# A transformer layer with int4 feed-forward weights: the first gate weights prepared one stage earlier, and the down-weight pieces of the last pair moved to the first pairs

## The reference

```python
x = x + layernorm(attention(layernorm(x)))        # x: 2048 tokens x 1024, 32 heads, 8 key/value groups
def ffn(x, gate_Wq, up_Wq, down_Wq, scales, zeros):
    # int4 weights, two to a word, one scale and one zero for 64 inputs
    Wg, Wu, Wd = dequantize(gate), dequantize(up), dequantize(down)
    g = einsum('bsh,ih->bsi', x, Wg)               # inter = 2752
    u = einsum('bsh,ih->bsi', x, Wu)
    return einsum('bsi,hi->bsh', silu(g) * u, Wd)
x = x + layernorm(ffn(layernorm(x)))
```

## Time and profile before

| | |
|---|---|
| median of 3 runs | 2761.49 us (2760.53 to 2762.55) |
| the profiled execution's own time | 2762.64 us |
| its span, first to last instruction | 2760.9 us |
| PE, busy | 2634.7 us, 95% |
| DVE, busy | 1602.5 us, 58% |
| POOL, busy | 1175.7 us, 43% |
| ACT, busy | 952.5 us, 34% |
| gate and up | from 1449 us to 2289 us |

### The profile page before, as it was taken

The page is one execution under the profiler, slowest core; times in us unless marked ns, Lnnn a source line. Parts: engine busy times, 40 slices in busy tenths (PEclk is TensorE's granted clock), DMA queues, the critical chain, the costliest instruction groups (busy, mean ns, idle before and its releaser), DMA issues. The chain is left out here.

```text
span 2760.9 us, 42122 instructions
## 1 busy us (share of the span) xinstructions
PE 2634.7 (95%) x17064; PEld 1116.0 (40%) x17064; DVE 1602.5 (58%) x1986; ACT 952.5 (34%) x1674; POOL 1175.7 (43%) x654
## 2 busy tenths in 40 slices
PE   6999899999999999988978999999999998999998
PEld 3445533333333333324443444444444443444443
DVE  6332778778787787815677688777777770101001
ACT  3111366666666666661112223233222220000000
POOL 0000177777777777781222334555555550100001
PEclk8999999999999999999988999999999998999999
DMA  4223101011010110003223222333333347332220
GB/s 171 81 76 97 30 17 30 22 40 30 17 30 24 38 30 2 1 1 145 91 76 107 91 76 90 112 106 111 101 113 108 106 152 254 110 105 71 71 71 30
DMA packets 180252, 209.67 MB, mean 76 GB/s; under 512 B 17649, under 2 KB 138737, under 8 KB 180081
## 3 DMA queue, kind: packets, MB, share of 16 engines
q1 hardware_dynamic: 175440, 198.11, 22.2%
q10 hardware_dynamic: 4640, 9.18, 0.9%
HBM read 146.01 MB, written 61.08 MB: 75 GB/s over the span
## 5 line engine op out<-in xcount | busy, mean ns | idle before, releaser
L734 POOL TENSOR_TENSOR c_prob<-c_prob 128x1024 f32<-128x1024 f32 (+1 forms) x288 | 604.7, 2118 | 518.2 <-ACT c_prob L632 515.7
L648 DVE TENSOR_REDUCE c_maxes<-c_s 128x2 f32<-128x1024 f32 (+3 forms) x640 | 645.6, 1057 | 196.2 <-PE c_s L488 196.2
L632 ACT ACTIVATE c_prob<-c_s 128x512 f32<-128x512 f32 (+1 forms) x1152 | 597.8, 571 | 299.4 <-PE c_s L510 185.3
L510 PE MATMUL c_s<-c_q,c_k 97*128 97x512 f16 (+3 forms) x1280 | 366.7, 352 | 10.1 <-ACT c_prob L632 1.7
L1292 PE MATMUL e_ps<-x_hi,e_w_hi 128*128 128x512 f16 x832 | 316.1, 380 | 15.3 <-DVE e_w_lo L1365 15.3
L1293 PE MATMUL e_ps<-x_lo,e_w_hi 128*128 128x512 f16 x832 | 315.9, 380 | 0.0
L1294 PE MATMUL e_ps<-x_hi,e_w_lo 128*128 128x512 f16 x832 | 315.8, 380 | 0.0
L525 PE MATMUL c_ctx<-c_prob,v_sb 128*32 128x512 f32 (+3 forms) x2560 | 293.4, 539 | 0.2 <-ACT c_c L621 0.2
L1677 POOL TENSOR_TENSOR e_w<-e_w,e_scales 128x1024 f32<-128x1024 f32 (+2 forms) x67 | 161.1, 2405 | 265.5 <-DVE e_w L1349 265.5
L77 DVE BATCH_NORM_STATS2 f_norm_stats<-f_yp 128x6 f32<-128x512 f32 x16 | 11.2, 698 | 416.1 <-PE f_yp L1823 416.1
L510 PEld LDWEIGHTS c_s<-c_q,c_k 97*128 97x128 f16 x1280 | 111.1, 97 | 345.2 <-ACT c_prob L632 298.7
(11 more groups left out here) (189 smaller groups left out, 3800.3 us busy)
## 6 DMA issues: line engine op xcount, KB each, us to landing
h_hi<-e_hh SPq DMA_DIRECT2D x84, 128.0 KB, 1.9
h_lo<-e_hl SPq DMA_DIRECT2D x84, 128.0 KB, 1.8
b_x<-L_attn_x SPq DMA_DIRECT2D x16, 512.0 KB, 6.2
c_q<-qk_hi SPq DMA_DIRECT2D x64, 128.0 KB, 3.1
d_x<-L_attn_x SPq DMA_DIRECT2D x16, 512.0 KB, 5.2
x_dram<-d_x SPq DMA_DIRECT2D x16, 512.0 KB, 2.6
f_x<-x_dram SPq DMA_DIRECT2D x8, 1024.0 KB, 7.2
out<-f_z SPq DMA_DIRECT2D x8, 1024.0 KB, 5.0
```

Of the source, the lines that this page charges most:

```text
L510: last = nc.tensor.matmul(S2[:, h % 2, at:at + w], K[:, g % 2, k * P:(k + 1) * P], Q[:, g % 2, b, h, q:q + w], start=True, stop=not diag)
L632: nc.scalar.activation(prob(g, s, 0, w)[:, h, :], S2[:, h % 2, 0:w], ACT.Exp, scale=exp_scale).then_inc(exp_done, 1)
L648: last = nc.vector.tensor_reduce(MAXES[:, g % 2, t // TPB, heads, t % TPB, u], S1[:, heads, at:at + w], AX.X, ALU.max)
L734: return nc.gpsimd.tensor_tensor(one, one, two, ALU.add)
```

## The change

It has two parts. First, task 0 (the first gate chunk) is loaded, unpacked, scaled and cut inside the projection stage, by the new class `Opening`, and the raw words of task 1 are loaded there too. Its buffers, and with them all the weight buffers of gate and up, now lie in the contexts' 2 x 32 KB, which fills them to the byte; the contexts' tensors therefore stay to the end, and in the down stage the down weights of chunks 4 to 19 lie there.

```diff
@@ SP, projection stage, ahead of the last store
+            sp.wait_ge(y_product, 2 * PAIRS)
+            for chunk in range(2):
+                opening.load(sp, chunk)
             store_rows(PAIRS - 1)
@@ DVE, body of the last pair, between cut_turned(i - 1) and x_norm
                     read_product(i + 1, 0)
+                else:
+                    dve.wait_ge(y_product, 2 * PAIRS)
+                    opening.unpack(dve)
                 x_norm.on_vector(...)
@@ DVE, after the last pair
             body(PAIRS - 1, last=True)
+            opening.trail(dve)
             cut_turned(PAIRS - 1)
@@ ACT, after the loop over pairs
+            opening.lead(act)
             cut_turned(PAIRS - 1)
@@ POOL, after the last residual
+            opening.scale(pool)
@@ gate and up: what is left of the start
-            for k in range(AT_START + 2):
+            for k in range(AT_START, AT_START + 2):
                 load(k)
-            for k in range(AT_START):
+            for k in range(1, AT_START):
                 unpack(k)
-            for name in weight_cuts(0):
+            for name in weight_cuts(0)[1:]:
                 cut(0, name)
```

```diff
-        places = [1] if p == 0 and q + 1 < PAIRS and q != PLAIN else [0, 1] if q + 1 == PAIRS else []
-        for place in places:
+        for place in {0: [1] if q + 1 < PAIRS and q != PLAIN else [],
+                      1: [0, 1] if role(q + 1) == "rest" else [0] if q < 3 else []}[p] if q + 1 < PAIRS else []:
@@
-                if role(q) != "up":
+                downs_first = role(q) != "up" or u in made_beside
+                if downs_first:
@@
-                    dve.wait_ge(cut_lo, cut_no[unit_of[k][0], weight_cuts(unit_of[k][0])[-1]])
+                    of, beside_p = unit_of[k]
+                    dve.wait_ge(cut_lo, cut_no[of + 1, "W1"] if kind == DOWN and beside_p and i == 0 else
+                                cut_no[of, weight_cuts(of)[-1]])
```

In the down stage the last part of the weights is loaded with three DMAs for each of high and low in place of two:

```diff
-                for buf, src in ((wd_hi, w_hi), (wd_lo, w_lo)):
+                for buf, over, src in zip(wd, wd_end, (w_hi, w_lo)):
+                    most = min(end, FIRST + MOST)
@@
                     if end == FULL:
-                        act.dma_start(buf[0:REST, FULL - FIRST, :], src[FULL * P:, :]).then_inc(w_loaded[i], 16)
+                        act.dma_start(over[:, 0:end - most, :], src[most * P:end * P, :]...).then_inc(w_loaded[i], 16)
+                        act.dma_start(over[0:REST, end - most, :], src[FULL * P:, :]).then_inc(w_loaded[i], 16)
```

More of the change, by code:

```diff
@@ L8 @@
+import math
 from contextlib import ExitStack
@@ L27 @@
 WS = 1024.0
+GS = WS / 4
 QS = 16.0
@@ L1097, in gate_and_up @@
     T_MADE = 3 * 2 * JC
-    raw_loaded = [sem(f"e_raw_loaded{s}") for s in range(2)]
-    unpacked, shifted, scaled, summed = (sem(f"e_{n}") for n in ("unpacked", "shifted", "scaled", "summed"))
-    cut_hi, cut_lo = sem("e_cut_hi"), sem("e_cut_lo")
+    raw_loaded, unpacked, shifted, scaled = opening.raw_loaded, opening.unpacked, opening.shifted, opening.scaled
+    cut_hi, cut_lo, summed = opening.cut_hi, opening.cut_lo, sem("e_summed")
     down_hi, down_lo, down_hi_stored, down_lo_stored = (
@@ L1265, in _ @@
                 for name in hs(q):
-                    if role(q) == "up" and name == hs(q)[2]:
+                    if not downs_first and name == hs(q)[2]:
                         for number in down_in.get(u, []):
@@ L1760, in project_down @@
         sb = lambda n, s, d=F32: ctx.enter_context(nc.sbuf_tensor("f_" + n, s, d))
-        wd_hi, wd_lo = (sb(n, [P, CHUNKS - FIRST, D], F16) for n in ("wd_hi", "wd_lo"))
+        MOST = T * c_hi.shape[1] // D
+        wd = [c[:].rearrange("p k t -> p (k t)").rearrange("p (c d) -> p c d", d=D) for c in (c_hi, c_lo)]
+        wd_end = [sb(n, [P, CHUNKS - FIRST - MOST, D], F16) for n in ("wd_end_hi", "wd_end_lo")]
+        assert APART < FIRST + MOST < FULL
         H_HI, H_LO = (sb(n, [P, 2, CHUNKS, BLOCK], F16) for n in ("h_hi", "h_lo"))
@@ L1772, in weights @@
         def weights(i, c):
-            return first.weights(i)[:, c] if c < FIRST else (wd_hi, wd_lo)[i][:, c - FIRST]
+            if c < FIRST:
+                return first.weights(i)[:, c]
+            return wd[i][:, c - FIRST] if c < FIRST + MOST else wd_end[i][:, c - FIRST - MOST]
         @block.sync
@@ L1876, in _ @@
             for i, (start, end) in enumerate(parts):
[L1877 to L1879 removed]
+                for buf, over, src in zip(wd, wd_end, (w_hi, w_lo)):
+                    most = min(end, FIRST + MOST)
+                    act.dma_start(buf[:, start - FIRST:most - FIRST, :],
+                                  src[start * P:most * P, :].rearrange("(c p) d -> p c d", p=P)).then_inc(w_loaded[i], 16)
                     if end == FULL:
[L1881 removed]
+                        act.dma_start(over[:, 0:end - most, :], src[most * P:end * P, :]
+                                      .rearrange("(c p) d -> p c d", p=P)).then_inc(w_loaded[i], 16)
+                        act.dma_start(over[0:REST, end - most, :], src[FULL * P:, :]).then_inc(w_loaded[i], 16)
             with act.Fori(0, 2 * ROUNDS) as r:
@@ L1890, in _ @@
                 nc.gpsimd.memset(h[REST:P, :, FULL, :], 0.0)
-            for w in (wd_hi, wd_lo):
-                last = nc.gpsimd.memset(w[REST:P, FULL - FIRST, :], 0.0)
+            for w in wd_end:
+                last = nc.gpsimd.memset(w[REST:P, FULL - FIRST - MOST, :], 0.0)
             last.then_inc(cleared, 1)
@@ L1923, in sandwich_layer @@
         build_constants(nc, ident, identb, causal, ones, sem)
+        c_hi, c_lo = (tensor(whole, n, [P, KC, T], F16) for n in ("c_hi", "c_lo"))
+        opening = Opening(nc, sem, (gate_q, gate_s, gate_z), c_hi, c_lo)
         with ExitStack() as context:
-            c_hi, c_lo = (tensor(context, n, [P, KC, T], F16) for n in ("c_hi", "c_lo"))
             with ExitStack() as attention:
```

68 lines of the change are left out of this document (54 added, 14 removed).

## The result

The changed kernel takes 2756.23 us (median of 15 runs, 2751.29 to 2758.72) against 2761.92 us for the kernel before, on the same chips: a ratio of 0.9977, with a 95% interval of 0.9970 to 0.9984. It is faster by 5.7 us (4.4 to 8.3 by the interval), where 13.3 were forecast. The profiled execution has a span of 2754.8 us against 2760.9.

A forecast was written before the change was run, and what follows sets the result against it. PE, busy 2634.7 of 2760.9 us, was taken as the bound, so only its idle time could be won. The terms -9.7 - 12.0 + 8.4 = -13.3 gave 2748.2 us, range 2740.5 to 2757.5.

The forecast's parts named there:

- Part 1: Start of gate and up: first weights ready early, PE starts 12.5 us sooner less 2.8, so 9.7 us won.
- the first gap: PE's wait for DVE's norm at the projection stage's last turn: grows by 2.8 us, from 12.90 to near 15.7.
- The last gap: PE's idle time between gate and up and down: 17.48 becomes 5.2 to 5.6, 12.0 us won.
- the slow first matmuls of the down stage: Start of the down stage: these matmuls stay slow, so no gain was counted there.
- the middle one: Pieces put beside early units, up to pair 5's W2: W2 comes 8.4 us later against PE (4.5 to 13).
- (0,1), (1,0) and (1,1): First units of gate and up: DVE's waits for PE absorb most added work, left 3.2 us (1 to 6).
- (2,0), full for small: Unit (2,0): a full piece in place of a small one costs 1.7 us.
- (2,1), one more full piece: Unit (2,1): one more full piece, partly covered by the 3.54 us wait for ACT's cut, costs 2.1 us.
- (3,0), full for small: Unit (3,0): a full piece in place of a small one costs 1.4 us.
- the gaps at P6 and P7: Unit (5,0): two PE gaps of some 11 to 12 us together, for S, then W2, in place of 3.49.
- a gap at the start of pair 3 or 4: Sign in PE's timeline: if a gap appears there, DVE's backlog is larger than forecast.
- the second rival: Little is absorbed: full pieces cost 5.1 us each, (1,1)'s two wait; W2 13 to 20 later, 2753 to 2760; chance 0.15.

The follow-up runs named there:

- e1: The kernel before plus the early opening alone, down pieces in their old places: 2750.4 us, ratio 0.9953.
- e3: The changed kernel with two of the four moved pieces beside (21,0) again, the other two beside (0,1) and (1,1): 2748.8 us, ratio 0.9952.
- e2: The changed kernel with the opening undone, task 0 prepared at the start of gate and up, pieces moved: 2765.5 us, ratio 1.0013.
- e9: The changed kernel with the pieces reordered only, five full ones first, then the four small ones: 2751.4 us, ratio 0.9965.
- e6: The changed kernel with pair 4's W2 cut ahead of the third token sum in unit (3,1): 2756.6 us, ratio 0.9981.
- e8: e10 with the order of pieces turned, four full ones first, then the small ones: 2739.2 us, ratio 0.9919.
- e10: e3 with the pieces' cuts behind the first gating in pair 2, old order of pieces: 2745.2 us, ratio 0.9945.
- e5: The changed kernel with token sums T4 made ahead of the cut of S in unit (4,1): 2754.9 us, ratio 0.9970.
- e11: The changed kernel with DVE's unpack of task 0 behind the last norm in the projection stage: 2754.6 us, ratio 0.9975.
- e4: The changed kernel with the piece's two cuts behind the first gating in pair 2, on DVE and ACT: 2750.1 us, ratio 0.9956.

## Why the prediction was wrong in its size

**Part 1 was right**: 9.7 us forecast. From PE's last projection product to the first matmul, gaps and turn together, were 12.90 + 3.67 + 15.30 = 31.9 us and are 15.68 + 3.68 + 2.64 = 22.0, so 9.9; the median of e1 gives 10.6. The added 2.78 in the first gap had been forecast as 2.8, but another instruction takes it, so that this number is right partly by luck. In the timeline of the changed kernel:

```profile
1436.99 5.77 POOL L925 TENSOR_TENSOR d_x<-d_x,d_y 128x1024 f32<-128x1024 f32 x2 [17.31 <-DVE d_y L95]
...
1439.82 0.41 DVE L1777 TENSOR_SCALAR c_hi<-c_lo 128x512 int32<-128x512 int32 x1
...
1440.60 3.24 DVE L1781 TENSOR_TENSOR c_lo<-c_hi,c_lo 128x1024 f32<-128x1024 int32 x1
```

The nibbles, at 0.41, were not held up; they came between POOL's two adds, which took 5.77 instead of 5.14 us. The subtraction behind them waited for the second add: 3.24 instead of 1.23. The Trainium skill (SBUF — State Buffer, "Who interferes with whom") has both cases, the two-port instruction and the one with two SBUF inputs, and says that the order of issue decides. The rows agree: the instruction that started behind the other is the longer one, POOL's second add behind the nibbles and the subtraction behind that add.

**The last gap was right**: 12.0 forecast, 12.31 measured. `First`'s loads stayed hidden: the last is issued by 2272.1, 12.5 us ahead of PE's start. That the slow first matmuls of the down stage would stay was not right, they gave 1.2 us.

**The step that failed is the middle one**, the cost of the pieces where they were put. "So W2 comes 8.4 us later against PE": it comes 14.6 later. Its items against the trace, from DVE's first unpack of each unit after the first matmul:

| unit | forecast | measured |
|---|---|---|
| (0,1), (1,0) and (1,1) | 3.2 | 3.4 |
| (2,0), full for small | 1.7 | 3.0 |
| (2,1), one more full piece | 2.1 | 5.5 |
| (3,0), full for small | 1.4 | 2.7 |
| sum | 8.4 | 14.6 |

More than half of the miss is the term of (2,1). It took the piece's cost and subtracted DVE's wait of 3.54 us for ACT's cut as cover. The piece's unpack did fill that wait, but the piece also goes through POOL and ACT before DVE can cut it, and DVE's queue stands until it is back, with the gatings behind: a wait of 3.33 opened in place of the one of 3.54. The cover was worth nothing, and the piece cost 5.5 us; e3, which takes it out, gives 5.3 back. In (2,0) the same wait of 3.33 stands where 0.58 and 1.24 stood before, with a small piece. In (3,0) DVE does not wait for ACT; a token sum of 0.68 us takes 2.84 beside POOL's scaling of the full piece, in the timeline of DVE in the changed kernel:

```profile
1583.49 2.84 DVE L1387 TENSOR_TENSOR c_lo<-x_lo 128x512 f32<-128x512 f16 x1
```

e1 and e2 exclude the later start as a cause, and e9 shows that it is no matter of DVE's total work, which is the same there with P7 4.8 us sooner. What each wait in pair 2 costs by itself is read from the timelines; only the piece of (2,1) as a whole was taken out.

What hung on it was right. The delay passes one for one to P7 (14.6 at (3,1) and 14.6 at P7), as the prediction had it, since no wait for PE lies behind; e6 showed that gaps on the way only share it. The forecast placed the gaps at P6 and P7; nearly half of it is paid earlier, for pair 4's W2. The prediction had named a gap at the start of pair 3 or 4 as the sign of a larger backlog, and this one lies close to that. The measured 2756.2 us lies in the upper end of the stated range, where it meets the second rival, "little is absorbed", 2753 to 2760 us. Half of that rival took place: the piece of (2,1) costs the 5.1 us it gives to a full piece and more. Its other half, a wait in (1,1) as in the last unit, did not: (1,1) cost 3.4.

One thing stays open: why DVE's wait for scales ahead of (2,1) is gone in the changed kernel and in e1.

## What to carry to other kernels

Work that is moved off the end must be priced where it lands, in its whole way through the engines and not in the busy time of the one engine that is short. A wait counts as cover only if the moved work does not end in a wait of its own: here 3.54 us were filled and 3.33 opened behind. Only the pieces of the very last unit were in the way here; two of the four could stay a unit earlier, and with two pieces fewer the large ones were better placed where DVE still waited for PE (e8 against e10). Before a moved item is called absorbed, find the last wait for the bounding engine ahead of the deadline, since nothing behind it absorbs anything.

## What was not expected of the hardware

DVE and POOL, both working from SBUF, take turns instruction by instruction: six sums of 0.68 us took 1.6 to 1.9 each beside POOL's sums, which went from 1.27 to 1.6 or 1.7 (e5). And a short DVE instruction that comes between two POOL instructions delays the second one, and DVE's next one is then the longer: 0.41 us against 3.24 in neighbouring rows, where the latter took 1.23 alone.

Executions of the same instructions differ by several microseconds in the clock granted in the first stretch of attention, 0.96 against 1.00 over 80 us, which moved everything behind by 2.9 us between the two profiled executions compared here, half of the whole effect of the change. The profiled executions of e1, e3 and e11 show 0.96 there too, those of e4 and e9 1.00.
